# Three edits at the start of a LoRA and masked-mixture kernel: A loaded in two halves, first LoRA products in another order, A_lo and W1 in other places on VectorE

## What is computed

```python
masked_w = weight * mask[None, :, :]
w_bot = jnp.einsum('bg,got->bot', y, masked_w)
x = x + jnp.einsum('bnt,bot->bno', x, w_bot) + bias0

out = jnp.einsum('btc,oc->bto', x, W_base) + b_base
h = jnp.einsum('btc,erc->bter', x, As)
lora = jnp.einsum('bter,eor,be->bto', h, Bs, w)
x = x + out + lora * 2
```

## Time and profile before

| | |
|---|---|
| Median of 3 runs | 57.18 us (57.12 to 57.25) |
| The profiled execution | 57.23 us |
| Its span, first to last instruction | 55.4 us |
| Busy: TensorE products | 51.7 us (93%) |
| Busy: VectorE | 42.1 us (76%) |
| Busy: ScalarE | 31.5 us (57%) |
| Busy: GpSimd | 31.2 us (56%) |
| Read from HBM, written | 7.54 MB, 4.19 MB |

### The profile page before, as it was taken

The page is one execution under the profiler, slowest core; times in us unless marked ns, Lnnn a source line. Parts: engine busy times, 40 slices in busy tenths (PEclk is TensorE's granted clock), DMA queues, the critical chain, the costliest instruction groups (busy, mean ns, idle before and its releaser), DMA issues.

```text
span 55.4 us, 997 instructions
## 1 busy us (share of the span) xinstructions
PE 51.7 (93%) x342; PEld 47.1 (85%) x342; DVE 42.1 (76%) x64; ACT 31.5 (57%) x52; POOL 31.2 (56%) x30
## 2 busy tenths in 40 slices
PE   2999999999999999999999999999999999999900
PEld 2988999999999888988998898899889889888800
DVE  0039999979596998999999999979929959805030
ACT  1949900447807889440999925970993950840800
POOL 4003400299980099999909999999966990000000
PEclk9999999999999999999999999999999999999999
DMA  0699999999999994000082540090054045049572
GB/s 0 133 392 335 373 366 389 419 418 425 408 396 417 417 393 169 9 0 0 0 306 78 222 169 0 15 364 0 6 195 183 0 185 194 0 179 382 197 284 95
DMA packets 5476, 11.79 MB, mean 213 GB/s; under 512 B 608, under 2 KB 1376, under 8 KB 5472
## 3 DMA queue, kind: packets, MB, share of 16 engines
q1 hardware_dynamic: 5184, 11.35, 54.6%
q10 hardware_dynamic: 288, 0.39, 1.9%
HBM read 7.54 MB, written 4.19 MB: 212 GB/s over the span
## 4 chain that ended last, share of the span: by engine, by line
PE 93%; DVE 1%; issue 0%
PE ps_out L441 13%; PE ps_out L483 13%; PE ps_out L445 13%; PE ps_out L449 13%; PE ps_merge L441 7%; PE ps_merge L445 7%; PE ps_merge L449 7%; PE ps_merge L522 6%; PE ps_lora L441 5%; PE ps_lora L445 5%; PE ps_lora L449 5%; DVE out_sb L432 1%; PE ps_lora L547 1%; DVE warm L310 0%
## 5 line engine op out<-in xcount | busy, mean ns | idle before, releaser
L189 POOL TENSOR_TENSOR W_lo<-W,W_hi 128x512 fp32r<-128x512 f32 x8 | 10.5, 1314 | 7.1 <-ACT W_hi L235 7.1
L342 DVE TENSOR_TENSOR x_lo<-x_sb,x_hi 128x1024 fp32r<-128x1024 f32 x8 | 12.7, 1584 | 0.0
L195 POOL TENSOR_TENSOR W_lo<-W,W_hi 128x512 fp32r<-128x512 f32 x6 | 10.9, 1824 | 0.0
L441 PE MATMUL ps_out<-x_hi,M_hi 128*128 128x512 f32 (+1 forms) x32 | 9.8, 388 | 0.0
L445 PE MATMUL ps_out<-x_lo,M_hi 128*128 128x512 f32 (+1 forms) x32 | 9.7, 384 | 0.0
L449 PE MATMUL ps_out<-x_hi,M_lo 128*128 128x512 f32 (+1 forms) x32 | 9.7, 384 | 0.0
L248 ACT ACTIVATE M_hi<-ps_merge 128x512 fp32r<-128x512 f32 x8 | 4.8, 597 | 8.0 <-PE ps_merge L449 8.0
L255 ACT ACTIVATE x_hi<-x_sb 128x1024 fp32r<-128x1024 f32 x8 | 8.4, 1053 | 0.0
L199 POOL TENSOR_TENSOR W<-W,ident 128x256 f32<-128x256 f32 x6 | 6.6, 1099 | 3.0 <-DVE x_lo L342 3.0
L357 DVE TENSOR_SCALAR out_sb<-ps_out,bias_sb 128x512 f32<-128x512 f32 x7 | 5.2, 747 | 3.5 <-PE ps_out L449 3.4
L264 ACT ACTIVATE out_sb<-ps_out,bias_sb 128x512 f32<-128x512 f32 x8 | 5.5, 685 | 3.9 <-PE ps_out L449 2.2
(11 more groups left out here) (50 smaller groups left out, 80.1 us busy)
## 6 DMA issues: line engine op xcount, KB each, us to landing
x_sb<-xT_dram SPq DMA_DIRECT2D x8, 512.0 KB, 10.2
outT_dram<-out_sb SPq DMA_DIRECT2D x15, 256.0 KB, 2.3
packs_sb<-packs_dram SPq DMA_DIRECT2D x7, 288.0 KB, 5.3
rows_sb<-rows_dram SPq DMA_DIRECT2D x1, 384.0 KB, 6.8
base_sb<-base_dram ACTq DMA_DIRECT2D x1, 256.0 KB, 3.6
outT_dram<-out_sb SPq DMA_DIRECT2D x2, 128.0 KB, 1.8
packs_sb<-head_dram SPq DMA_DIRECT2D x1, 192.0 KB, 3.4
packs_sb<-rest_dram SPq DMA_DIRECT2D x1, 160.0 KB, 3.6
```

What stands on the lines that cost most here:

```text
L189: pool.tensor_tensor(W1_lo[:, b % W1BUF], W1[:, b % W1BUF], W1_hi[:, b % W1BUF].bitcast(f32), ALU.subtract).then_inc(w1lo_done, 1)
L195: pool.tensor_tensor(W0_lo[:, b % 2], W0[:, b], W0_hi[:, b % 2].bitcast(f32), ALU.subtract).then_inc(w0lo_done, 1)
L342: nc.vector.tensor_tensor(x_lo[:, b % XBUF], x_sb[:, b], x_hi[:, b % XBUF].bitcast(f32), ALU.subtract).then_inc(xlo_done, 1)
L441: nc.tensor.matmul(out, hi_l, hi_r, start=(n == 0), stop=False)
```

## The change

The A load, 268 columns, becomes two: condition, biases and the first 128 columns of A, then the other 128, each with its own semaphore. The second is issued behind the first on SyncE's queue, and all later loads of that queue stand one place further back. ScalarE makes A_hi of batch 0 in two halves, one for each load. `lora_first()` takes the place of `lora(0)` and `lora(1)`: the same twelve products, but the first hi-by-hi product of batch 1 comes third. `WARM` goes from 28 to 24. On VectorE only five A_lo are made at the start; the sixth goes behind `low_bias`, the seventh and eighth behind `w1` of the main loop. Two W1 come ahead of the first mask product, and the others are one place earlier among them.

```diff
@@ constants
-    WARM = 28
+    AHEAD = 5
+    WARM = 24
@@ sync
-            sp.dma_start(lora_sb[:, 0:OBT], factors_A).then_inc(lora_arrived, 16)
+            sp.dma_start(lora_sb[:, 0:OA1], factors_A0).then_inc(A0_arrived, 16)
+            sp.dma_start(lora_sb[:, OA1:OBT], factors_A1).then_inc(A1_arrived, 16)
@@ scalar
-            act.wait_ge(lora_arrived, 16)
-            for b in range(NB):
+            act.wait_ge(A0_arrived, 16)
+            nc.scalar.activation(A_hi[:, 0, 0:H], A_er[:, 0:H], ACT.Copy, scale=cond_er[:, 0:1]).then_inc(ahi_done, 1)
+            act.wait_ge(A1_arrived, 16)
+            nc.scalar.activation(A_hi[:, 0, H:C], A_er[:, H:C], ACT.Copy, scale=cond_er[:, 0:1]).then_inc(ahi_done, 1)
+            for b in range(1, NB):
                 a_hi(b)
@@ vector
             def a_lo(b):
-                dve.wait_ge(ahi_done, b + 1)
+                dve.wait_ge(ahi_done, b + 2)
...
-            for b in range(NB):
+            for b in range(AHEAD):
                 a_lo(b)
...
+            a_lo(AHEAD)
             m_lo(1)
             split_x_lo(1)
...
                 if b + 3 < NB:
                     w1(b + 3)
+                if b + AHEAD < NB:
+                    a_lo(b + AHEAD)
                 if b + 1 < NB:
                     split_x_lo(b + 1)
@@ tensor
+            def lora_first():
+
+                def term(b, j, left, right, first=False, last=False):
+                    return nc.tensor.matmul(ps_lora[b][:, j, :], left[:, b, j * P:(j + 1) * P], right[:, :],
+                                            start=first, stop=last)
+
+                pe.wait_ge(bhi_done, 1)
+                pe.wait_ge(ahi_done, 1)
+                term(0, 0, A_hi, B_hi, first=True)
+                pe.wait_ge(blo_done, 1)
+                term(0, 0, A_hi, B_lo)
+                pe.wait_ge(ahi_done, 3)
+                term(1, 0, A_hi, B_hi, first=True)
+                pe.wait_ge(alo_done, 1)
+                term(0, 0, A_lo, B_hi, last=True)
+                term(0, 1, A_hi, B_hi, first=True)
+                term(0, 1, A_hi, B_lo)
+                term(0, 1, A_lo, B_hi, last=True).then_inc(lora_mm, 1)
+                term(1, 0, A_hi, B_lo)
+                pe.wait_ge(alo_done, 2)
+                term(1, 0, A_lo, B_hi, last=True)
+                term(1, 1, A_hi, B_hi, first=True)
+                term(1, 1, A_hi, B_lo)
+                term(1, 1, A_lo, B_hi, last=True).then_inc(lora_mm, 1)
...
-            lora(0)
-            lora(1)
+            lora_first()
```

More of the change, by code:

```diff
@@ L3, with conditional_residual_kernel @@
 from contextlib import ExitStack
-def conditional_residual_kernel(nc: bass.Bass, head: bass.AP, rest: bass.AP, packs: bass.AP, factors_A: bass.AP,
+def conditional_residual_kernel(nc: bass.Bass, head: bass.AP, rest: bass.AP, packs: bass.AP, factors_A0: bass.AP,
+                                factors_A1: bass.AP,
                                 factors_B: bass.AP,
@@ L34, in conditional_residual_kernel @@
     W1BUF = 4
-    WARM = 28
+    AHEAD = 5
+    WARM = 24
     assert packs.shape == (NQ - 1, P, PACKW)
     OB0, OB1, OA, OBT = NB, NB + NT, NB + 2 * NT, NB + 2 * NT + C
+    OA1 = OA + H
     cut = MIXW + C
@@ L374, in _ @@
                                            op0=ALU.mult, op1=ALU.subtract).then_inc(blo_done, 1)
-            dve.wait_ge(lora_arrived, 16)
-            for b in range(NB):
+            dve.wait_ge(A0_arrived, 16)
+            dve.wait_ge(A1_arrived, 16)
+            for b in range(AHEAD):
                 a_lo(b)
             nc.vector.tensor_tensor(bias_sum[:, :], bias0, bias1, ALU.add).then_inc(fixed_done, 1)
-            dve.wait_ge(fixed_done, 1)
+            dve.wait_ge(base_done, NT)
+            w1(0)
+            w1(1)
             w0(0)
             w0(1)
-            dve.wait_ge(base_done, NT)
-            w1(0)
             w0(2)
-            w1(1)
             w0(3)
+            w1(2)
             w0(4)
-            w1(2)
             w0(5)
+            w1(3)
             w0(6)
-            w1(3)
             w0(7)
+            dve.wait_ge(fixed_done, 1)
             dve.wait_ge(w0_done, NQ)
@@ L450, in product @@
                 return mm
-            def lora(b):
[L454 to L458, removed]
+            def lora_first():
[20 more added lines that the diff above has]
+                term(1, 1, A_lo, B_hi, last=True).then_inc(lora_mm, 1)
+            def lora(b):
+                pe.wait_ge(alo_done, b + 1)
+                pe.wait_ge(w1_done, b - 1)
                 if b == 5:
@@ L463, in lora @@
                     mm = product(ps_lora[b % 2][:, j, :],
-                                 [(A_hi[:, b, cols], A_lo[:, b, cols], B_hi[:, :], B_lo[:, :])],
-                                 lo_ready=(alo_done, b + 1),
-                                 mid_ready=(blo_done, 1) if b == 0 and j == 0 else None)
+                                 [(A_hi[:, b, cols], A_lo[:, b, cols], B_hi[:, :], B_lo[:, :])])
                 mm.then_inc(lora_mm, 1)
@@ L598 @@
               "packs": packs[:, first:].reshape(P, NQ - 1, -1).transpose(1, 0, 2),
-              "factors_A": lora[:, :-C], "factors_B": lora[:, -C:], "base": halves(base.T), "rows": rows, "xT": xT}
+              "factors_A0": lora[:, :-C - P], "factors_A1": lora[:, -C - P:-C], "factors_B": lora[:, -C:], "base": halves(base.T), "rows": rows, "xT": xT}
     arrays = {n: np.ascontiguousarray(a) for n, a in arrays.items()}
```

4 lines of the change are left out of this document (2 added, 2 removed).

## The result

The changed kernel took 59.48 us (median of six runs, 58.59 to 59.74), beside 57.3 us for the kernel before in the same comparison. The ratio is 1.031, with a 95% interval of 1.022 to 1.040: slower by some 1.8 us, where 57.5 was predicted and 58.6 was the top of the range. The medians take every execution, but the ratios leave out those that lie over 1.5% above the fastest of their kernel (37 of 67 in the kernels with 24 warm-up products, three of the six of after among them, 28 of 110 in the other kernels of the experiments, with 28 or 32, and 7 of 115 of the kernel before), so a ratio cannot show a loss that falls on some executions only. Where traces are compared I go by spans, since 2.5 us lay around the span of the profiled execution of after, and 1.8 around that of before.

A forecast was written before the change was run, and what follows sets the result against it. TensorE was taken as the bound, 93% of the chain of waits. 57.23 - 0.07 (split A load) - 0.11 (W1 order) + 0.47 (late A_lo) = 57.52, given as 57.5 us; range 57.0 to 58.6.

The forecast's parts named there:

- Part 3, A_lo(5): VectorE behind low_bias: A_lo(5) goes before GpSimd's W_lo(2), total delay with A_lo(6) 0.40 to 0.62 us, stall 0.47 at apply(2).
- the forecast's outcome: VectorE's A_lo(5) goes ahead of GpSimd's W_lo(2) and takes about 0.48 us; time 57.5 us, chance 0.48.
- rival 1: GpSimd's W_lo(2) goes first, A_lo(5) waits, M_lo(1) 1.08 us late, stall 1.33, time 58.4 us; chance 0.15.
- Part 3, A_lo(6): VectorE between W1(4) and x_lo(2): delay 0.40 us, less slack 0.15 at apply(2); lower bound of the stall 0.25.
- A_lo(7): VectorE, one batch after A_lo(6): finds slack, since x_lo(3) is ready over 1 us before its use.
- Part 1: Start, A load in two halves and first products reordered: gain 0.07 us (0.18 gained to 0.33 lost); later loads cost zero.
- Part 2: End of the ramp, W1 before the mask products: the 0.11 us stall at the merge goes; early W1 and W0 otherwise worth nothing.
- Rival 3, the clock: Start: TensorE's pause before the first product delays the faster pace to 9.4 us, +1.3 us, time 58.8; chance 0.05.

The follow-up runs named there:

- the run that turned it: The changed kernel with GpSimd's W0_lo(2) held until A_lo(5) is done, so VectorE goes first: ratio 1.017, median 58.70 us.
- with one tensor: The kernel before with A in two loads from one HBM tensor, first products reordered, 28 warm-up products: ratio 1.001, median 57.48 us.
- with 28 warm-up products: The kernel before with A in two loads and first products reordered, 28 warm-up products instead of 24: ratio 1.005, median 58.00 us.
- The pairs: Without against with the split A load: W1 early and three A_lo late, 1.020 against 1.033; same with A_lo(5) at the start, 0.991 against 1.009.
- part 2 alone: The kernel before with only VectorE's W1 moved ahead of the mask products: ratio 0.995 (0.992 to 0.998).
- part 3 undone: The changed kernel with all eight A_lo made at the start: ratio 1.0002 (0.996 to 1.004).
- part 3 alone: The kernel before with five A_lo at the start, A_lo(5) behind low_bias, A_lo(6) and (7) behind W1 of the main loop: ratio 1.024.
- the pairs above: Three kernels with 24 warm-up products, each beside its counterpart with 28: medians slower by 0.65, 0.35 and 0.20 us.

## Why the prediction was wrong, point by point

**Part 3, A_lo(5): the step that failed.** The forecast let A_lo(5) go first, at about 0.48 us, with a delay of 0.62 us for all that follows and a stall of 0.47. The runs showed W_lo(2) going first and A_lo(5) at 1.59 us, and the main stretch longer by 1.49. The prediction had both outcomes and a price for each, and saw that the two instructions became ready within 0.05 us of each other. It then gave the forecast's outcome 0.48 and the other 0.15. Nothing in its argument settled which engine would go first, so that was too little. The timelines of VectorE and GpSimd of before do hold a hint:

```profile
20.56 0.59 DVE L404 TENSOR_SCALAR low_bias<-lora_sb,A_bias 128x8 f32<-128x8 f32 x1
```

```profile
19.49 1.63 POOL L199 TENSOR_TENSOR W<-W,ident 128x256 f32<-128x256 f32 x2 [3.02 <-DVE x_lo L342]
```

`low_bias`, in front of the slot, takes 0.59 us for eight elements a partition, and ends within 0.03 us of GpSimd's diagonals (21.15 and 21.12): it looks as if it had itself waited for GpSimd. Two engines that are held and freed by the same access would be free together each time, with GpSimd's next instruction standing ready. In all four traces with A_lo(5) in this slot, VectorE's record starts 4 to 17 ns ahead of GpSimd's, and in all four GpSimd ran first. That the tie is made by the lock is argued from these records; that the order is worth 0.9 us is shown by the run that turned it.

The Trainium skill (SBUF — State Buffer, "Who interferes with whom") calls the shared pair of ports an exclusive lock, and says that the order of issue decides who blocks. The lock agrees with 1.59 us beside 1.30; the order can't be read off the start times, which had VectorE ahead.

**The price of rival 1 was mis-sized.** It was 58.4, with M_lo(1) 1.08 late (1.07 measured). But I carried the delay to `apply(2)` as one stall of 1.33 and named none at `lora(5)`, where by the forecast's slack of 0.18 it would already have been 0.90. In fact the first of the two last dots, which had lain beside a GpSimd diagonal in before (0.97 us), fell beside a W_lo and took 1.52; the second kept its 1.39, and x_lo(1) took 0.22 less. `bias_sb` was ready 1.39 late and `lora(5)` paid 1.2 of it; `apply(2)` added 0.38. Sum 1.58, not 1.33. "More if the dots meet GpSimd worse" was in the text, and not in the number.

**Part 3, A_lo(6): right.** 0.25 forecast for it alone, 0.26 measured. With A_lo(5) going first the forecast had 0.47, and the run about 0.65. **A_lo(7)** cost nothing, as said (main stretch 37.30 with it late or early).

**Part 1: the gain right, its cover wrong.** The landing (3.86 against 3.98; 2.3 to 2.8 us after its issue in the eight traces) and the gain (0.07, bounds to 0.18; 0.16 at the first mask product where the spacing changed at the same time) hold. The step that failed is "the packs and x wait for bandwidth, not for issue, and TensorE reaches them later than they land, so zero". In all eight traces with both halves of A on SyncE's queue the head load took 4.3 to 4.9 us, and in the eleven with one A load 3.4 to 3.6. (The rest load behind it took 4.2 to 5.4, against mostly 3.6 to 4.0; but with unchanged loads it was late in two traces too, 5.0 and 5.3.) From 4.0 to 5.2 us the engines moved this much in after, and in before:

```profile
DMA packets 179, 0.25 MB, mean 211 GB/s; under 512 B 18, under 2 KB 148, under 8 KB 179
```

```profile
DMA packets 276, 0.41 MB, mean 342 GB/s; under 512 B 38, under 2 KB 166, under 8 KB 276
```

though SyncE's queue kept them busy for as large a share of that time (93.6% in after, 92.5% in before, where ScalarE's queue had another 13.0%): fewer packets, each slower. The base load on ScalarE's queue gained what the head load lost in part: 2.8 to 3.0 us in the same eight traces, 3.4 to 3.9 in the eleven. Why is open, though it is not the place in memory. By how much the late loads cost depends on when TensorE reaches them. In before's order `lora(2)` waits for W1(0) until 10.2 in any case, which hides most of the delay in one trace (10.40 with one tensor) and not in another (11.16 with 28 warm-up products, where packs were awaited). With all three parts it shows. The pairs give 1.020 against 1.033, and 0.991 against 1.009. But beside part 2 alone, part 1 costs 0.5% (0.995 against 1.000), no more than by itself, so W1(0) is not the whole of it; what else makes the difference is open.

**Part 2: the right gain, and a larger one that I had excluded.** The 0.11 at the second merge half is there in after (0.10) and with part 3 undone (0.14), but not with part 2 alone, where the diagonal met GpSimd. "VectorE has a backlog at 8 us, but TensorE waits for none of it, so the early W1 and W0 are worth nothing" failed: it was true of the trace of before, one execution, in which the spacing changed late. When TensorE is faster, W1(0) is the next limit, and the ratio of 0.995 measures it.

**Rival 3, the clock: it happens, and I can't say how often.** In after's own trace there was no loss: the granted clock was 1.00 as before, and the spacing fell to 0.12 earlier. The ratios for 24 and 28 warm-up products show none either. But the trace of the whole change with six A_lo at the start has the rival's case:

```profile
7.22 4.67 PE L514 MATMUL ps_out<-packs_sb 128*128 128x128 f32 x32
11.64 0.36 PE L452 MATMUL ps_lora<-B_hi,A_hi 128*128 128x256 f32 x1
```

From the first mask product to `lora(2)` pass 4.42 us instead of before's 3.49, with no load awaited. The last eight of the first LoRA products and the first nine mask products came 0.21 us apart, so the pace changed at about 9.2 us (the rival had 9.4). The first merge product started at 16.64, 1.27 later than in after (the rival had +1.3). This kernel's profiled execution took 58.95 us, near its median of 58.98. So the rival's case is real, though no run shows how much of after's time it is. What makes the pace change late in some executions isn't shown either; the medians of the pairs above point at the four missing warm-up products. The Trainium skill (TensorE: Matmul & The Clock Gate, "What's actually happening") has activity release the throttle, and says that the point of the change varies. Here the same start got the faster pace at 5.1 us in one execution and at 6.3 in another.

**The sum.** Main stretch +1.49 by the trace, start +0.14, together 1.64; the ratio says 1.8, with an interval of 1.3 to 2.3. By kernels: part 3 alone 1.024 and part 2 -0.005 make 1.019, and the two together measured 1.020. Part 1 beside them, 0.011 to 0.013, is the difference to the whole, so the total of 1.031 to 1.033 does not confirm it. Rival 1's own 58.4 lay inside the range; what took the time beyond 58.6 is its mis-sized stall and part 1's loads. What stays open is why packets slow down when A comes in two loads.

## What to carry over

Before a VectorE instruction with two inputs in SBUF goes into a gap, read GpSimd's list at that moment: if the two become ready together, price both orders alike, or fix the order with a semaphore. An instruction far too long for its size (0.59 us for eight elements) may be a sign that the gap lies at such a place. And a limit that nothing waits for in one trace is only covered: moving two covers at once (W1 and the loads) can uncover what neither shows alone, so test parts in pairs, too.

## What was not expected of the hardware

- The tie at 20.98: in four kernels the record of VectorE's A_lo starts 4 to 17 ns before that of GpSimd's W_lo, and GpSimd ran first each time, for 1.29 or 1.30 us, with A_lo at 1.59 or 1.60. Why GpSimd won is open.
- The same waiting is paid by quite different instructions of VectorE: 0.59 us for `low_bias` (eight elements), 0.76 for the diagonal (0.42 alone), 1.52 for a dot, 1.92 for an x_lo (1.22 alone).
- With A loaded in two halves on one queue, the head load (192 KB) took 4.3 to 4.9 us in all eight traces, 3.4 to 3.6 in the eleven with one A load, while the base load (256 KB) on the other queue took 2.8 to 3.0 instead of 3.4 to 3.9.
- The pace of 0.12 us a product began between 5.1 and 6.9 us in most traces, at about 9.2 in one and 9.8 in another, with 1.00 as the granted clock where the pace was 0.21 as well.
